# Attention products one slot further behind the scores, with four buffers instead of three, and the normalisation chain one slot later

## The reference

```python
x = x + layernorm(attn(layernorm(x)))     # 16 heads of 64, q and k l2-normalised, q times exp(scale)
x = x + layernorm(ffn(layernorm(x)))      # silu(x w1) * (x w2) -> gelu(h1) -> gelu(h2) -> w3
# attn: sim = q k^T; softmax(sim) v; heads joined; @ w_out + b_out
```

## Time and profile before

| | |
|---|---|
| Time, median of 3 runs | 1752.87 us (1748.74 to 1756.21) |
| The profiled execution's own time | 1754.2 us, span 1752.3 us |
| TensorE busy | 1703.1 us, 97% of the span |
| VectorE busy | 1181.1 us, 67% |
| ScalarE busy | 1009.6 us, 58% |
| GpSimd busy | 461.1 us, 26% |
| Mean granted TensorE clock | 0.992 of full speed |

### The profile page before, as it was taken

How to read it: one execution, slowest core, us unless ns; L and a number is a source line. 1 busy time by engine, 2 the same in 40 slices (tenths; PEclk the granted TensorE clock), 3 DMA queues, 4 the chain that set the end, 5 groups by cost and what they waited for, 6 DMA issues and landing times.

```text
span 1752.3 us, 24703 instructions
## 1 busy us (share of the span) xinstructions
PE 1703.1 (97%) x8608; PEld 1421.6 (81%) x8608; DVE 1181.1 (67%) x2026; ACT 1009.6 (58%) x1350; POOL 461.1 (26%) x563
## 2 busy tenths in 40 slices
PE   7999999999999999999999998999999999999998
PEld 5788888888888888888888776888888888888877
DVE  6777877877877878877877874545454545544454
ACT  4877877877877777777777765322323141323231
POOL 4433533533533533533533520000000000000000
PEclk8999999999999999999999998999999999999999
DMA  4466466456466466466466562400000000000000
GB/s 148 106 140 162 110 139 165 109 139 155 105 140 156 104 144 153 103 144 152 103 149 159 139 163 73 166 13 25 0 25 1 24 1 24 1 25 1 24 1 25
DMA packets 76700, 162.75 MB, mean 93 GB/s; under 512 B 28256, under 2 KB 28640, under 8 KB 76576
## 3 DMA queue, kind: packets, MB, share of 16 engines
q1 hardware_dynamic: 67216, 127.98, 31.1%
q10 hardware_dynamic: 8352, 29.50, 5.6%
q0 software_dynamic: 1008, 3.67, 0.5%
HBM read 68.97 MB, written 20.19 MB: 51 GB/s over the span
## 4 chain that ended last, share of the span: by engine, by line
PE 74%; DVE 12%; DMA 5%; issue 4%; ACT 3%; POOL 2%; SPq 1%; DVEq 0%; ACTq 0%; POOLq 0%
PE bank L1133 14%; PE pair L1210 13%; PE pair L1211 13%; PE bank L1061 10%; PE bank L1147 4%; PE pair L1115 4%; PE pair L1116 4%; DVE Pl L759 4%; PE pair L1200 3%; PE pair L1201 3%; PE bank L1090 2%; PE bank L1227 2%; PE bank L1228 2%; DVE work L775 1%; DMA rows<-Rp 1%
## 5 line engine op out<-in xcount | busy, mean ns | idle before, releaser
L1210 PE MATMUL pair<-hh,f 128*128 128x512 f32 x1024 | 399.3, 390 | 0.7
L1211 PE MATMUL pair<-hl,f 128*128 128x512 f32 x1024 | 398.5, 389 | 0.0
L1133 PE MATMUL bank<-Ph,V 128*128 128x512 f32 x1024 | 368.6, 401 | 20.9 <-DVE Pl L759 11.8
L534 ACT ACTIVATE P<-pair,sh 128x1024 f32<-128x1024 f32 x256 | 286.4, 1119 | 152.3 <-PE pair L1116 137.9
L759 DVE TENSOR_TENSOR Pl<-P,Ph 128x1024 fp32r<-128x1024 f32 x256 | 315.6, 1233 | 10.8 <-ACT Ph L539 10.8
L584 ACT ACTIVATE hr<-pair,ct 128x512 f32<-128x512 f32 x128 | 88.3, 690 | 357.6 <-PE pair L1211 357.6
L1061 PE MATMUL bank<-w,xh 128*128 128x512 f32 (+1 forms) x1016 | 281.4, 339 | 4.1 <-DVE turned L753 3.9
L539 ACT ACTIVATE Ph<-P 128x1024 fp32r<-128x1024 f32 x256 | 271.8, 1062 | 8.1
L1133 PEld LDWEIGHTS bank<-Ph,V 128*128 128x128 f32 x1024 | 194.5, 190 | 81.3 <-issue 34.4
L1210 PEld LDWEIGHTS pair<-hh,f 128*128 128x128 f32 x1024 | 192.2, 188 | 43.8 <-DVE hl L873 3.5
L1211 PEld LDWEIGHTS pair<-hl,f 128*128 128x128 f32 x1024 | 192.2, 188 | 39.7
(11 more groups left out here) (126 smaller groups left out, 2639.5 us busy)
## 6 DMA issues: line engine op xcount, KB each, us to landing
stack<-turned SPq DMA_DIRECT2D x127, 384.0 KB, 4.6
stack<-turned SPq DMA_DIRECT2D x127, 256.0 KB, 4.8
work<-rows SPq DMA_DIRECT2D x128, 128.0 KB, 3.0
raw<-in_h ACTq DMA_DIRECT2D x16, 512.0 KB, 4.3
xr<-in_h ACTq DMA_DIRECT2D x16, 512.0 KB, 3.6
f<-raw ACTq DMA_DIRECT2D x12, 512.0 KB, 5.1
f<-raw SPq DMA_DIRECT2D x10, 512.0 KB, 9.3
xr<-in_x SPq DMA_DIRECT2D x8, 512.0 KB, 5.5
```

Source lines behind the costliest of these rows:

```text
L534: e.activation(M.P[:, i % 2, :], M.SB[i % 2][:, :], ACT.Exp, bias=M.sh[:, h:h + 1]).then_inc(S["exp"])
L1133: d = e.matmul(M.OB[:, :], v, p[:, u % 3, j * 512:(j + 1) * 512], start=jt == 0 and m == 0, stop=jt == 3 and m == 2)
L1210: e.matmul(ps, w, M.hh[src][:, k, :].bitcast(to), start=k == 0, stop=False)
L1211: d = e.matmul(ps, w, M.hl[src][:, k, :].bitcast(to), start=False, stop=k == KH - 1)
```

## The change

`LAG = 3` replaces the 2 in TensorE's program: the products with V of slot i - 3 now stand in slot i. Ph and Pl get a fourth buffer. To pay for it the spread reciprocals `Rb` and the normalised result `on` go from two buffers to one, the weights' staging buffers are reused once, and the counting instructions write over their own input instead of into a scratch tile. ScalarE's evacuations move from odd slots to the following even ones. The chain of the reciprocals moves by one slot: `invert` from 4n + 7 to 4n + 8, `normal` from 4n + 10 - n % 2 to 4n + 11 - n % 2, and `o_high` and `o_low` with it. `outp(Q)` stays in slot 8Q + 15. At the start, the transposes of q of pair 1 use the bank OB, so that they do not wait for the scaling of the second quad's first tile; that tile is summed and scaled before the output weights are split; pair 1's `turned` halves are made in slot 1 instead of 0. In the last sequence, the slots of the last pairs' chain are set anew.

```diff
+LAG = 3
@@ bank_plan @@
-            order += [(("Tk", pair_of(i)), i), (("Tq", pair_of(i)), i)]
+            order.append((("Tk", pair_of(i)), i))
+            if i:
+                order.append((("Tq", pair_of(i)), i))
@@ turn_bank @@
-    return M.FB[j] if n == 0 else M.G[PLAN["Tk" if j else "Tq", n][0]][:, :]
+    if n == 0 or n == 1 and j == 0:
+        return M.OB[:, :] if n else M.FB[j]
+    return M.G[PLAN["Tk" if j else "Tq", n][0]][:, :]
@@ slots of the chain @@
+def invert_slot(n):
+    return NU - 3 if n == NP - 3 else 4 * n + 8
 def normal_slot(n):
-    return {NP - 4: NU - 4, NP - 3: NU + 1, NP - 2: NU + 1, NP - 1: NU + 5}.get(n, 4 * n + 10 - n % 2)
+    return {NP - 4: NU - 3, NP - 3: NU + 1}.get(n, 4 * n + 11 - n % 2)
 def low_slot(n):
-    return NU - 2 if n == NP - 4 else normal_slot(n) + 1
+    return normal_slot(n) + 1
@@ act_program @@
-        q.wait_ge("pv", u - 2)
-        e.activation(M.Ph[:, u % 3, :], M.P[:, u % 2, :], ACT.Copy).then_inc(S["ph"])
+        q.wait_ge("pv", u - 3)
+        e.activation(M.Ph[:, u % 4, :], M.P[:, u % 2, :], ACT.Copy).then_inc(S["ph"])
...
-        if i % 2 and 0 <= i // 2 - 1 < NG:
-            evacuate(i // 2 - 1)
+        if i % 2 == 0 and 0 <= i // 2 - 2 < NG:
+            evacuate(i // 2 - 2)
@@ vector_program, count_piece @@
-        e.tensor_scalar(M.junk[:, :], words[:, 0:2048:2], 0.0, None, ALU.not_equal, ALU.add,
+        e.tensor_scalar(words[:, 0:2048:2], words[:, 0:2048:2], 0.0, None, ALU.not_equal, ALU.add,
@@ vector_program, start @@
+    head_sums(NT)
     for t in range(NT):
         first_scale(t, 1)
+    head_scale(NT)
     split_wo(0)
     split_wo(1)
-    head_sums(NT)
     split_w(7)
-    head_scale(NT)
@@ vector_program, loop: behind p_low(i - 1) @@
+        for n in pairs(low_slot, i):
+            o_low(n)
+        for n in pairs(normal_slot, i):
+            if n % 2:
+                normal(n)
@@ vector_program, loop: behind the head_scale calls @@
+        for n in pairs(normal_slot, i):
+            if n % 2 == 0:
+                normal(n)
+        for n in pairs(invert_slot, i):
+            if r == 0:
+                invert(n)
@@ tensor_program @@
-        if 0 <= i - 2 < NU:
-            values(i - 2)
+        if 0 <= i - LAG < NU:
+            values(i - LAG)
@@ attention_memory @@
-    M.Ph = sb("Ph", [128, 3, 1024], f32r)
-    M.Pl = sb("Pl", [128, 3, 1024], f32r)
-    work = sb("work", [128, 8, 512], f32)
-    M.Ev, M.Rb, M.on = work[:, 0:4, :], work[:, 4:6, :], work[:, 6:8, :]
+    M.Ph = sb("Ph", [128, 4, 1024], f32r)
+    M.Pl = sb("Pl", [128, 4, 1024], f32r)
+    work = sb("work", [128, 6, 512], f32)
+    M.Ev, M.Rb, M.on = work[:, 0:4, :], work[:, 4, :], work[:, 5, :]
```

More of the change, by code:

```diff
@@ L316, in sync_program @@
     load_x(0)
-    for n in range(8):
-        e.dma_start(stage[n], M.wqkv[:, n % 2, n // 2, :]).then_inc(S[f"wld{n}"], 16)
+    for n in (0, 1, 2, 3, 4, 5, 7):
+        load_w(n)
     for k in range(2):
@@ L328, in sync_program @@
         i32_, pb = i % 32, i // 32 - 1
-        if i % 2 == 0 and 0 <= i // 2 - 2 < NG:
+        for n in pairs(invert_slot, i):
+            store_rec(n)
+        for n in pairs(invert_slot, i - 1):
+            if n % 2:
+                spread_rec(n)
+        if i % 2 and 0 <= i // 2 - 2 < NG:
             take_sums(i // 2 - 2)
+        for n in pairs(invert_slot, i - 1):
+            if n % 2 == 0:
+                spread_rec(n)
         if i % 8 == 6 and pair_of(i - 1) is not None:
             stack(pair_of(i - 1), 1)
-        if i % 4 == 0 and 0 <= i // 4 - 2 < NP:
-            spread_rec(i // 4 - 2)
         if 0 <= pb < B - 1 and i32_ == 16:
@@ L628, in act_program @@
             v_high(values_of(i))
-        if pair_of(i) is not None:
+        if i and pair_of(i) is not None:
             turn_high(pair_of(i), 1)
             turn_high(pair_of(i), 0)
+        if i == 1:
+            turn_high(1, 1)
+            turn_high(1, 0)
         if i == NU:
@@ L932, in vector_program @@
             x_low(b + 1, 0)
-        if r == 3 and 0 <= n - 2 < NP:
-            invert(n - 2)
+        for n in pairs(invert_slot, i):
+            if r == 4:
+                invert(n)
         if 0 <= i - 1 < NU:
             p_low(i - 1)
+        for n in pairs(invert_slot, i):
+            if r == 5:
+                invert(n)
         if i == NU - 7:
@@ L964, in vector_program @@
             v_low(values_of(i))
-        if pair_of(i) is not None and i != NU - 8:
+        if i and pair_of(i) is not None and i != NU - 8:
             turn_low(pair_of(i), 1)
             turn_low(pair_of(i), 0)
+        if i == 1:
+            turn_low(1, 1)
+            turn_low(1, 0)
         for u in tiles_of(i - 1) if i else []:
             head_scale(u)
-        if i == normal_slot(NP - 4):
-            normal(NP - 4)
-        if r == 3 and 0 <= n - 3 < NP and low_slot(n - 3) == i:
-            o_low(n - 3)
-        if r == 7 and 0 <= n - 2 < NP:
-            invert(n - 2)
+        for n in pairs(normal_slot, i):
+            if n % 2 == 0:
+                normal(n)
+        for n in pairs(invert_slot, i):
+            if r == 0:
+                invert(n)
         if quad_of(i) is not None and i < BRANCH_AT:
@@ L986, in vector_program @@
     o_low(NP - 3)
-    normal(NP - 2)
     for b in range(B):
@@ L1004, in vector_program @@
                 if b == 0 and n == 0 and m == 3:
+                    normal(NP - 2)
+                if b == 0 and n == 0 and m == 5:
                     o_low(NP - 2)
@@ L1132, in values @@
             for m, (v, p) in enumerate(((both, M.Ph), (both, M.Pl), (low, M.Ph))):
-                d = e.matmul(M.OB[:, :], v, p[:, u % 3, j * 512:(j + 1) * 512], start=jt == 0 and m == 0,
+                d = e.matmul(M.OB[:, :], v, p[:, u % 4, j * 512:(j + 1) * 512], start=jt == 0 and m == 0,
                              stop=jt == 3 and m == 2)
@@ L1262, in rest @@
     def rest(rounded):
-        for i in range(BRANCH_AT, NU + 2):
+        for i in range(BRANCH_AT, NU + LAG):
             attention(i)
@@ L1343, in attention_memory @@
     flat = work[:, :, :].rearrange("p a b -> p (a b)")
-    M.stage = ([M.P[:, i, 0:768] for i in range(2)] + [flat[:, i * 768:(i + 1) * 768] for i in range(5)]
+    M.stage = ([M.P[:, i, 0:768] for i in range(2)] + [flat[:, i * 768:(i + 1) * 768] for i in (0, 1, 2, 3, 0)]
                + [M.y[:, :, :].rearrange("p a b -> p (a b)")[:, 0:768]])
```

47 lines of the change are left out of this document (25 added, 22 removed).

## The result

The changed kernel takes 1826.25 us (1824.77 to 1828.12, 4 runs), the kernel before beside it 1751.59 us (1748.74 to 1756.21). The ratio is 1.042, 95% interval 1.040 to 1.045. The forecast was 1788 us with a range up to 1812: right in sign, half the size. The profiled executions stand at 1824.77 and 1754.2 us, 70.6 us apart, where the sum had 35.5.

A forecast was written before the change was run, and what follows sets the result against it. TensorE, busy for 97% of the span, was taken as the bound. Its terms, -15.6 + 35.1 + 14 + 8 - 5 - 1 = +35.5 us on 1754.2, gave 1789.7, stated as 1788 us for the median; range 1762 to 1812.

The forecast's parts named there:

- What bounds the kernel: Whole kernel: TensorE is busy for 97% of the span, so only its waits and its clock change the time.
- the order at the quad's end: VectorE in r7: nl now stands behind ss and the Pl of r6, where before it stood in r6 ahead of ss.
- the new wait: Output projection at each quad's end: TensorE waits 1.17 us for nl, thirty times, +35.1 us.
- The projection's waits in sum: Output projection waiting for nl: +35.1 us over thirty quads, +14 and +8 more where VectorE is behind.
- The values' waits for Pl, -15.6: Products with V, steady attention from 66 to 1035 us: lag three removes all 23 waits, -15.6 us.
- the cost of the evacuations: Evacuations moved to even slots: OB is free in time, 0, at most +0.3 us in quads with a late exponential.
- the step before: VectorE's work newly ahead of nl in quads ending in slots 143 and 135: 3.25 us, including 1.40 for normal.
- 22 us for the late quads: Quads ending in slots 143 and 135, seven each: projection waits beyond the ordinary 1.17 us, +14 and +8 us.
- the rival at 0.15: Finishing quad: TensorE's clock halves once per sequence behind a wait of about 3 us, +20 us, 1808 us; chance 0.15.
- VectorE beside GpSimd, up to 7 us in the range: Slots 140 to 142: Pl or normal beside GpSimd's additions may lose another microsecond per sequence, 7 us, left to the range.
- The start, -5: Start-up: the 3.77 us wait goes, slot 2's tile starts at 36.6 us; -7 to -2 us, taken as -5.
- The end, -1: End of attention: the 3.47 us evacuation wait for normal of pair NP - 4 stays; +3 to -12 us, taken as -1.

The follow-up runs named there:

- ea: The kernel before with only the odd pairs' nl moved, to r7 behind Pl instead of r6; lag two stays: 1777.24 us, ratio 1.014.
- en: The changed kernel with the even pairs' normal early in r3's list, ahead of ss, instead of last behind the scaling: 1784.38 us, ratio 1.019.
- enb: The changed kernel with two edits to VectorE's order, even pairs' normal early in r3 and nl ahead of Pl in r7: 1753.83 us, ratio 1.000.
- ep: The changed kernel with a third buffer P, paid for by Pl's fourth; exp waits for one Pl less: 1826.90 us, ratio 1.043.
- ec: The changed kernel with ScalarE evacuating OB between exp and Ph in the r6 slots, instead of behind both: 1837.69 us, ratio 1.049.
- es: The changed kernel with the start's edits on TensorE, ScalarE and VectorE taken back; SyncE's loads keep their new order: 1824.87 us, ratio 1.042.
- eb: The changed kernel with VectorE making nl ahead of Pl in r7, instead of behind it: 1784.52 us, ratio 1.017.
- ex: The changed kernel with normal back in r2 and r5, nl in r3 and r6, odd pairs' reciprocals spread in their inversion's slot: 1829.46 us, ratio 1.046.

## Why the prediction was wrong

- *What bounds the kernel, the order at the quad's end, the new wait*: right. 30 waits for nl; 1.08 (`ea`, `en`) to 1.29 us where nothing else is late (forecast 1.17).
- *The projection's waits in sum*: forecast 35.1 + 14 + 8 = 57.1, measured 56.0. That is partly luck. The finishing and statistics quads came out lower (2.43 and 1.94 for 3.2 and 2.3), because another wait stood ahead and took a share; slot 31's came out higher.
- *The values' waits for Pl, -15.6*: gone as forecast, but not gained. With VectorE's order repaired, the design with lag three is no faster than the kernel before (`enb` 1.000), and with the finishing work spread and the end repaired too, the two are level.
- **The step that failed** is the cost of the evacuations, "0, with at most +0.3 us in the quads where the exponential is late". They wait 21.2 us in the steady part. Behind it stands a gap in the step before: I put the first pair's `normal` "from free time into this stretch" and counted it in two of four quads only, against nl alone. It comes in every quad, ahead of the counting in slot 31's, and delays Pl, by that the exponential, and by that the evacuation. The two waits must be priced as one: VectorE's work from r4 to nl. `en`, which takes out nothing but this move, loses 15 of the 21 us of evacuation waits and 15 of the projection's 54. That it runs at 1784.4 us, within 4 us of the forecast, is partly luck: the forecast had 22 us for the late quads, 17 to 18 of it for the very `normal` that `en` takes away, so by its own terms it would have put `en` near 1770. That the two waits have one cause is shown by `ep` and `ec`, where one went and the other grew.
- *What the sum missed*: 36.1 us between 35.5 and 71.6. The evacuations are 21.2 of them, the clock 10.2, the end 6.1 and the start 5.5 (what the start gained by its clock stands under the clock); the other terms are smaller and together -6.9.
- *The clock*: the rival at 0.15 was true in kind. Seven finishing quads and more have a stretch at 0.50, each 3.4 us, not the 6.7 us that I priced; about +10 us in all, not +20. The Trainium skill ("TensorE: Matmul & The Clock Gate", section "Part 1: The HAM clock gate") says that the clock falls behind idleness; the trace agrees, at 652.5 us. I set its condition at one wait of about 3 us. Two waits of 1.61 and 2.27 us with products between them did it too, and in `en` a single one of 1.95 us, so the condition was too high.
- *VectorE beside GpSimd, up to 7 us in the range*: not seen in sum. `Pl` and `normal` together are busy for 412.5 us, against 409.9 before.
- *The start, -5*: the reading was right, slot 2's tile starts at 36.66 us (forecast 36.6) behind a wait of 3.11, and slot 8 starts 3.6 us sooner; but `es` shows 0 for the whole. *The end, -1*: +5.1, of which 2.4 are a wait of 5.9 instead of 3.5 us for an evacuation.

## What to carry to other kernels

When a change moves a job on an engine that has no free time in some stretch, add up all that this engine does between its last free moment and the result that the bottleneck waits for. Do this in each kind of stage, and look at where the job runs in the trace, not at the slot in whose list it stands: `normal` was moved by one slot, and by that crossed from free time into a full stretch, for 42 us. Two waits of the bottleneck that go back to the same late engine are one cost: taking away the first shows nothing (here a third buffer, 0 us), while less work ahead of the second does show (`eb`, 42 us). And the deeper pipeline gained nothing here: it hid the late Pl from the products, but VectorE had as much to do as before, and TensorE waited for its next result instead.

## What the runs showed of the hardware

- Waits of TensorE of about 2 us can bring the clock down, and their length alone does not settle it. A wait of 1.1 us in each quad left it at 1.00 from 70 to 1083 us (`ea`). 1.61 and 2.27 us within six us brought it to 0.50 for 3.4 us in each of seven sequences of the changed kernel; the same two waits did so in six of seven in `es`. With 0.64 and 1.84 us there (`en`, start to start) it stayed at 1.00, but for the last sequence. There it fell right behind the first wait alone. In `ep` it fell behind a single wait of 2.04 us (at 442 us), and not behind one of 2.69 (at 198 us). The last sequence of `en`, the wait and then the stretch behind it (from:to, length, TensorE's busy time, granted clock, DMA share, GB/s):

```profile
1029.95 0.47 PE L1173 MATMUL bank<-Ph,V 128*128 128x512 f32 x1 [1.95 <-ACT work L572]
```

```profile
1030.45:1037.25 6.80, 5.97 (x23) 0.50 0.99 221
```

- A reciprocal of 128 x 8 spread over two transfers by way of memory takes 4.5 us from its own start to its use, more than a slot of 3.1 us (`ex`); stored at 714.82, read back from 716.24, landed at 719.00, used at 719.08.
